# Attention on one core: sums of two units ago spread between the scores, own scores in four-row pieces, buffers in halves

## What is computed

```
q, k, v = 1x1 convolutions (256 x 256) of layernorm(x), as (n, 16 heads, 16 channels, row i, column w)
own      = sum_c q[c,i,j] * k[c,i,w]                     # per row i: 128 x 128
relative = Gq * sum_c q[c,i,j] * rq[c,j,w] + Gk * sum_c k[c,i,j] * rk[c,j,w]
weight   = softmax over w of (own + relative) / 16       # per head, image and row i: 128 x 128
out      = sum_w weight[i,j,w] * (Gv1 * v[c,i,w]) + sum_w weight[i,j,w] * (Gv2 * rv[c,j,w])
x = x + 1x1 convolution of out; then a mixture of 64 experts, each on its 8 best tokens
```

## Time and profile before

| | us |
|---|---|
| median of 3 runs | 8304.97 (8296.95 to 8308.47) |
| the profiled execution's own time | 8291.75 |
| its span | 8290.0 |
| TensorE busy in the span | 7187.2 (87%) |
| VectorE busy | 5176.6 (62%) |
| ScalarE busy | 4856.3 (59%) |
| GpSimd busy | 2457.0 (30%) |
| mean granted clock of TensorE | 0.749 of 2.4 GHz |

### The profile page before, as it was taken

One profiled execution on the slowest core, in us unless ns is written; L12 is line 12 of the kernel. 1 busy time (PEld: TensorE's weight loads), 2 busy tenths in 40 slices (PEclk: granted clock), 3 DMA queues, 4 the chain that ended last, 5 costly groups with the idle time before them and its releaser, 6 DMA issues. The chain is left out here.

```text
span 8290.0 us, 275612 instructions
## 1 busy us (share of the span) xinstructions
PE 7187.2 (87%) x106442; PEld 6044.4 (73%) x106442; DVE 5176.6 (62%) x20646; ACT 4856.3 (59%) x11427; POOL 2457.0 (30%) x1235
## 2 busy tenths in 40 slices
PE   4999999799999999999999899999999966766738
PEld 3555555689988888898899898898888932332338
DVE  5444444366666666666666666666666768988830
ACT  1444444577777777777777777777777733333410
POOL 0000000243443443444434444434434432322210
PEclk7999999666666666666666666666667688988855
DMA  7555555565655665655556656656656576766522
GB/s 217 203 203 204 204 204 197 113 112 100 112 103 98 113 107 101 107 99 107 101 106 112 102 100 109 109 99 110 105 100 109 92 232 203 265 201 202 208 74 99
DMA packets 1721071, 1148.11 MB, mean 138 GB/s; under 512 B 1143009, under 2 KB 1506145, under 8 KB 1703329
## 3 DMA queue, kind: packets, MB, share of 16 engines
q1 hardware_dynamic: 1530336, 842.56, 48.1%
q10 hardware_dynamic: 188352, 285.27, 9.3%
q0 software_dynamic: 1024, 2.09, 0.1%
HBM read 708.04 MB, written 421.56 MB: 136 GB/s over the span
## 5 line engine op out<-in xcount | busy, mean ns | idle before, releaser
L787 POOL TENSOR_TENSOR att_scores<-att_scores,att_inverse 128x1024 f32<-128x1024 f32 x1024 | 1966.8, 1934 | 2951.7 <-DVE att_inverse L722 2951.7
L660 ACT ACTIVATE att_scores<-att_scores,att_negmax 128x128 f32<-128x128 f32 x8192 | 2509.2, 399 | 67.6 <-issue 67.6
L737 DVE CUSTOM_DVE_ANT_0 att_scores<-att_ps,att_scores 128x128 f32<-128x128 f32 x8192 | 1780.8, 286 | 1066.7 <-PE att_ps L573 957.5
L560 PE MATMUL att_ps<-att_qk,att_rs 32*128 32x64 f32 x32768 | 1793.2, 380 | 155.6 <-ACT att_scores L652 114.2
L560 PEld LDWEIGHTS att_ps<-att_qk,att_rs 32*128 32x128 f32 x32768 | 1698.6, 299 | 196.2 <-ACT att_scores L652 142.5
L573 PE MATMUL att_ps<-att_own 16*128 16x128 f32 x16384 | 1541.6, 405 | 231.3 <-issue 224.1
L573 PEld LDWEIGHTS att_ps<-att_own 16*128 16x128 f32 x16384 | 1416.2, 300 | 268.9 <-issue 264.4
L652 ACT ACTIVATE att_scores<-att_ps 128x1024 f32<-128x1024 f32 x1024 | 992.4, 1021 | 1044.3 <-PE att_ps L560 1044.3
L720 DVE TENSOR_REDUCE att_total<-att_scores 128x8 f32<-128x1024 f32 x1024 | 1233.7, 1205 | 70.7 <-issue 70.7
L594 PE MATMUL att_ps<-att_scores,att_rv 128*16 128x64 f32 x32768 | 1249.6, 334 | 11.0 <-issue 10.8
L594 PEld LDWEIGHTS att_ps<-att_scores,att_rv 128*16 128x16 f32 x32768 | 1193.6, 127 | 24.5 <-issue 13.1
(11 more groups left out here) (146 smaller groups left out, 5276.0 us busy)
## 6 DMA issues: line engine op xcount, KB each, us to landing
qk<-proj_qk_out ACTq DMA_DIRECT2D x64, 2048.0 KB, 8.5
att_qk<-qk SPq DMA_DIRECT2D x512, 256.0 KB, 6.7
att_own<-qk SPq DMA_DIRECT2D x2048, 64.0 KB, 2.5
proj_x<-in_x_dram SPq DMA_DIRECT2D x128, 512.0 KB, 4.3
v_t<-proj_v_out ACTq DMA_DIRECT2D x64, 1024.0 KB, 11.3
att_vt<-v_t SPq DMA_DIRECT2D x128, 512.0 KB, 5.5
att_v<-att_att_v SPq DMA_DIRECT2D x512, 128.0 KB, 4.2
att_r<-att_att_r SPq DMA_DIRECT2D x512, 128.0 KB, 3.5
```

The costliest lines, as they stand in the source:

```text
L560: last = pe.matmul(ps[:, 4 + g, jj * IU:(jj + 1) * IU], rs[32 * g:32 * g + 32, t * JB + jj, :], qk[b][32 * g:32 * g + 32, :, t * JB + jj], ...
L660: last = act.activation(scores[v][:, i, :], scores[v][:, i, :], ACT.Exp, bias=negmax[v][:, i:i + 1], scale=-1.0)
L737: last = dve.tensor_tensor_reduce(out=scores[v][:, i, :], in0=ps[:, 2 * (p % 2) + r // 4, (r % 4) * W:(r % 4 + 1) * W], in1=scores[v][:, i ...
L787: pool.tensor_tensor(scores[v][:, rows, :], scores[v][:, rows, :], inverse[v][:, rows].unsqueeze(2).broadcast_to([P, PR, W]), ALU.mult).th ...
```

## The change

Every unit now has the same order of work on TensorE, and the sums in it are those of the unit two before. For each quarter t of a unit:

own piece 4t; relative round t, first half; v fill t, first half; own 4t+1; relative, third quarter; r fill t, first quarter; v fill t, second half; own 4t+2; relative, last quarter; r fill t, second and third quarter; own 4t+3; r fill t, last quarter.

An own piece now has 4 rows, all in the row group p % 4, and uses bank p % 2. Relative scores move to banks 2 to 5; all v sums go through bank 6 (read by VectorE alone) and all r sums through bank 7 (read by ScalarE). Both banks are cleared once at the start. `vt`, `att_v` and `att_r` are split in two halves with semaphores of their own, `rv` loads and their semaphores in four. Exponentials run two pieces behind the own scores, sums of exponentials two groups of eight rows behind. The scaling of the tables by GpSimd moves to later places, and `att_r` is stored as 8 runs of 16 columns in place of 4 of 32 (JT).

The core of the diff (left out: declarations, the load helpers and the unit's calls in SyncE's code at the start and the end):

```diff
-PR = 8
+PR = 4
 PIECES = IU // PR
+SR = 8
+SPIECES = IU // SR
-JT = JG
+JT = JG // 2
+STORES_G = JG // JT
...
# SyncE
             def unit(h, k, u, started, left):
                 if started >= 1:
                     sp.wait_ge(own_done, PIECES * u)
                     load_own(h, k, 1)
-                if started >= 2:
-                    store(*before(h, k, 2), u - 2)
-                if started >= 1:
-                    ph, pk = before(h, k, 1)
-                    later(sp, v_done, FILLS * (u - 1))
-                    load_v(ph, pk)
...
                 if left >= 2:
                     sp.wait_ge(rel_done, ROUNDS * u + ROUNDS)
                     load_qk(*after(h, k, 2))
+                if started >= 3:
+                    store(*before(h, k, 3), u - 3, 1)
+                if started >= 2:
+                    later(sp, v_done, FILLS * (u - 2))
+                    ph, pk = before(h, k, 2)
+                    load_v(ph, pk, 1)
+                    if pk == 0:
+                        later(sp, r_done, FILLS * (u - 2))
+                        load_rv(ph, 2)
+                        load_rv(ph, 3)
+                if k == UPH - 1 and left >= 1:
+                    load_relative(h + 1, 1)
...
                 if left >= 1:
                     sp.wait_ge(own_done, PIECES * u + PIECES // 2)
                     load_own(*after(h, k, 1), 0)
+                if started >= 2:
+                    store(*before(h, k, 2), u - 2, 0)
+                if started >= 1:
+                    ph, pk = before(h, k, 1)
+                    later(sp, v_done, FILLS * (u - 2) + FILLS // 2)
+                    load_v(ph, pk, 0)
...
# TensorE
             def own_scores(u, p):
+                half, g = p // (PIECES // 2), p % G
...
                 later(pe, added, PIECES * u + p - 1)
-                for r in range(4):
-                    for gg in range(2):
-                        g = 2 * (p % 2) + gg
-                        at = block16 * 4 + r
-                        last = pe.matmul(ps[:, g, r * W:(r + 1) * W], ...
+                for r in range(PR):
+                    at = (p // G) % (HROWS // 16) * PR + r
+                    last = pe.matmul(ps[:, p % 2, r * W:(r + 1) * W], ...
...
+            def unit(u, v, now, ahead, late, sums):
+                b, o = (v - 2) % BUFS, (v + 1) % 2
+                for t in range(FILLS):
+                    if now:
+                        own_scores(u, 4 * t)
+                    if ahead:
+                        relative(u + 1, o, t, (0, 1))
+                    if sums:
+                        sums_with_v(u - 2, b, t, (0, 1))
+                    if now:
+                        own_scores(u, 4 * t + 1)
+                    if ahead:
+                        relative(u + 1, o, t, (2,))
+                    if sums:
+                        sums_with_r(u - 2, b, t, (0,))
+                        sums_with_v(u - 2, b, t, (2, 3))
+                    if now:
+                        own_scores(u, 4 * t + 2)
+                    if ahead:
+                        relative(u + 1, o, t, (3,))
+                    if sums:
+                        sums_with_r(u - 2, b, t, (1, 2))
+                    if now:
+                        own_scores(u, 4 * t + 3)
+                    if sums:
+                        sums_with_r(u - 2, b, t, (3,))
...
# ScalarE
+            BEHIND = 2
+            def unit(u, v, now, ahead, late, sums):
+                for p in range(PIECES):
+                    if p < BEHIND:
+                        if late:
+                            exp_piece(u - 1, (v - 1) % BUFS, PIECES - BEHIND + p)
+                    elif now:
+                        exp_piece(u, v, p - BEHIND)
+                    if p % 4 == 3:
+                        if ahead:
+                            read_relative(u + 1, (v + 1) % BUFS, p // 4)
+                        if sums:
+                            read_r(u - 2, p // 4)
...
# VectorE
+                for p in range(PIECES):
+                    if now:
+                        add_and_largest(u, v, p)
+                    if sums and p % 4 == 2:
+                        read_v(u - 2, p // 4)
+                    if p % 2 == 1:
+                        k = p // 2 - BEHIND
+                        if k >= 0 and now:
+                            sums_of(u, v, k)
+                        elif k < 0 and late:
+                            sums_of(u - 1, (v - 1) % BUFS, SPIECES + k)
...
# GpSimd
-                        if k == UPH - 2 and not last and p in (2, 4):
-                            scale_relative(h + 1, p // 2 - 1)
+                        if k == UPH - 2 and not last and p == 6:
+                            scale_relative(h + 1, 0)
+                        if k == UPH - 1 and not last and p == 2:
+                            scale_relative(h + 1, 1)
```

More of the change, by code:

```diff
@@ L512, in unit @@
                     load_qk(*after(h, k, 2))
[L513 to L514 removed]
+                if started >= 3:
[10 more added lines that the diff above has]
+                    load_relative(h + 1, 1)
+                if k == UPH - 2 and left >= 2:
                     load_gain(h + 1)
@@ L577, in sums_with_v @@
[L577 to L581, removed]
+                for r in range(PR):
+                    at = (p // G) % (HROWS // 16) * PR + r
+                    last = pe.matmul(ps[:, p % 2, r * W:(r + 1) * W], own[half][32 * g:32 * g + HD, 1, at, :], own[half][32 * g:32 * g + HD, 0, at, :],
+                                     start=True, stop=True, tile_position=(32 * g, 0))
@@ L585, in sums_with_v @@
                                          start=True, stop=True, tile_position=(0, 32 * g))
[L586 to L593, removed]
-                        last = pe.matmul(ps[32 * g:32 * g + HD, bank, jj * IU:(jj + 1) * IU], rv[:, g * JG + b * JB + jj, :], scores[v][:, :, g * JG + b * JB + jj],
-                                         start=True, stop=True, tile_position=(0, 32 * g))
-                last.then_inc(r_done, 1)
@@ new lines, in sums_with_v, with sums_with_r @@
+                if 3 in quarters:
+                    last.then_inc(v_done, 1)
+            def sums_with_r(u, v, b, quarters):
+                if 0 in quarters:
+                    pe.wait_ge(rv_loaded[b], (u // UPH) * 16 + 16)
+                    if b == 0:
+                        pe.wait_ge(normed, SPIECES * u + SPIECES)
+                    later(pe, r_read, FILLS * u + b)
+                for x in quarters:
+                    for jj in range(x * JB // 4, (x + 1) * JB // 4):
+                        for g in range(G):
+                            j = g * JG + b * JB + jj
+                            last = pe.matmul(ps[32 * g:32 * g + HD, 7, jj * IU:(jj + 1) * IU], rv[:, j, :], scores[v][:, :, j],
+                                             start=True, stop=True, tile_position=(0, 32 * g))
+                if 3 in quarters:
+                    last.then_inc(r_done, 1)
@@ L640, in _ @@
+            pe.wait_ge(cleared, 1)
             for t in range(ROUNDS):
-                relative(0, 0, t)
+                relative(0, 0, t, (0, 1, 2, 3))
             units(pe, unit)
```

275 lines of the change are left out of this document (92 added, 183 removed).

## The result

The changed kernel took 9953.34 us (median of 4 runs, 9938.02 to 9991.55) beside 8300.96 us for the kernel before (4 runs, 8291.03 to 8308.47): 1.1998 times as long, 95% interval 1.1961 to 1.2035. That is 1652 us more, where 3060 were forecast. The direction and the range were right; the likeliest case, a low clock throughout, did not come. What came is the second rival, the swinging clock, priced at 10,020 and given a chance of 0.14.

The account below looks back on a forecast made before the run. TensorE was taken to bound the attention stage. At the low clock 128 units of 63.1 us plus 120 us of table waits make 8197 against 5137, +3060 us, so 11,365 us; range 8500 to 12,000.

Parts of the forecast that it names:

- the second rival: Attention clock swings, high half the time: 52.6 us a unit, +1716 us, 10,020 us; chance 0.14.
- Step 3: Attention clock: without long unbroken runs of sums it stays low (0.50); called the large term.
- Step 1: Own scores, each piece in one row group: records wait in turn, 25.2 us a unit low, 14.7 high.
- Step 2: Sums in sixteenths: 32 tiling changes a unit at 0.20 us low, 0.15 high, so 6.4 or 4.8 us.
- Step 4: TensorE's whole attention unit: 60.3 us low, 39.4 high with tiling changes; 63.1 and 42.2 with start-up and stalls.
- Step 5: ScalarE and VectorE swap v-sum reads in attention; both stay covered by TensorE: no added time.
- step 6: Relative scores' wait for ScalarE's read (100.6 us) goes: at most 0.8 us a unit, left out.
- step 8: SyncE's transfers, 38 DMAs a unit for 29: 7 to 8 us more, covered by a 63 us unit.
- step 9: Combine stage reads relative sums in 512-byte runs instead of 1024: taken as 0, at worst 60 us.
- Step 7: GpSimd's relative-table scaling at head's end stalls TensorE: two waits of about 4 us, 15 times, 120 us.
- The first rival: High clock holds through attention: 42.2 us a unit, +385 us, 8690 us; chance 0.12 (high and slower).
- The faster rival: High clock holds and loads run ahead hide tiling changes: 38.0 us a unit, -273 us, 8030; faster chance 0.14.

Follow-up runs that it names:

- e5: Changed kernel with sums dealt evenly, a quarter of v and of r sums behind each own piece; 11427.02 us, 1.3777 times the kernel before.
- e1: Changed kernel with each four-row own piece spread over two row groups, one bank each; 8773.01 us, 1.0578 times the kernel before.
- e3: Kernel before with each own piece issuing four matmuls of one row group, then four of the other, not alternating; 9031.67 us, ratio 1.0898.
- e7: Changed kernel with eight-row own pieces over two row groups and sums in eighths, 16 tiling changes a unit; 7900.54 us, 0.9529 times the kernel before.
- e6: Changed kernel with GpSimd's table scaling before pieces 4 and 1 instead of 6 and 2; 9805.48 us, 1.1815 times the kernel before.
- e8: e7 with the second half of values loaded first on SyncE and tables scaled earlier; 7759.19 us, 0.9356 times the kernel before.

## Why the prediction was right and where it failed

- **Step 3, the clock, failed.** It said that in the spread order the clock stays low for good. It was high 38% of the attention's time, about as much as before (36%). The stated range held the result because it reached over both clocks, not because the clock was understood. Taking 62.3 and 39.0 us a unit and the 370 us of stalls over 1 us (92, counted in the trace), (6783 - 370) = 62.3 n + 39.0 (128 - n) gives n = 61 low ones: half the units' work at either level, which is the rival priced at 10,020. The reasoning went wrong in making a long unbroken run of sums the condition: the changed order still has 48 records of r sums around one own piece at the end of each quarter, and with them the clock does rise (e5 takes them away and the forecast time comes, 11,427 beside 11,365). Half the units at the high level instead of none is 67 x 23.3 = 1560 us; the miss in time was 1412. Two smaller errors make about the difference: a low unit 2.0 us dearer, 256 us over 128, and stalls of 370 us for the 358 and 120 taken.
- **Step 1, one row group, was right.** 210 to 214 ns between records low and 107 to 112 high stand beside 197 and 115. e1 and e3 show that it costs time, 1180 and 746 us with what the clock did beside it. Its reason was only partly right. "Nothing runs beside it, since matmuls start in order" is refuted by the rows at 3003.04 and 3003.32: relative scores, which the program has behind the piece, start before its last own records do. Five slip in there; over the trace it is mostly three to seven where relative scores follow a piece and none where sums do, 3.6 in the mean. The trace of the kernel before had it too, which the prediction overlooked: two relative records start at 3138.18 and the last own record of the piece before them at 3138.39.
- **Step 2, changes of tiling, was right in kind and a little low:** 0.26 and 0.18 us measured, 0.20 and 0.15 taken, inside its bounds, 31.5 a unit. The Trainium skill's drain (TensorEngine Tiling (Array Packing), section Key Properties) was no overstatement.
- **Step 4, the sum, was right** (62.3 and 39.0 for 60.3 and 39.4), in part by luck, since errors cancel: own records and changes were dearer, v sums took 42 ns and r sums 31 ns at the low clock where 48 and 36 were taken, and relative scores slipped in beside own ones.
- **Step 5, step 6, step 8 and step 9 were right:** TensorE waits 0.7 us in all for `v_t` and for no store, 9.2 us for ScalarE's reads, and what stands behind the attention is as long as before (1625.5 us). Step 8 holds at 53 us a unit only: at e7's 37 the same queue costs 223.8 us.
- **Step 7, the tables, was mis-sized:** 182.3 us in 30 waits of 6.1, where 30 waits of 4 were taken. The scaling's 3.60 us was counted, and not what GpSimd still has to normalise ahead of it; e6, with less ahead of it, has 76.9 us.
- **The first rival (high clock holds, 8690)** did not come, with the high level in only half of the units. The faster rival (8030) needed changes under 0.11 us: refuted by 0.18. The gain of e7 and e8 comes with half as many changes.

## What to carry to other kernels

Price TensorE's work at both granted levels and then ask separately what share of the time each will have; the two lie far apart, here 23 us of 62 a unit, and a forecast that puts every unit on one level misses by that for each unit on the other. In the versions run here, spreading sums between score pieces paid only with pieces in two row groups, few changes of tiling and no waits for VectorE: with 16 changes a unit 5 to 6% faster than the kernel before, with 32 in two groups 4 to 6% slower, with 32 in one group 20% slower. After each gain read the waits again, since loads that 53 us a unit hid are late at 37.

## What the runs showed of the hardware that was not expected

- TensorE busy 7961.37 of 8268 us, with float32 own scores in one row group at a time and short runs of sums, is granted 0.50 in the mean of the stage (e5).
- A matmul of a free row group starts ahead of an earlier one that waits for its own: the relative record at 3003.04 before the own record at 3003.25. The Trainium skill (TensorE: Matmul & The Clock Gate, section The mechanism) has matmuls start strictly in the program's order; these rows disagree.
- Sums with relative v (128x64 moving) cost 30 to 36 ns a record at either clock, while own, relative and v records take little more than half the time at the high one (213 and 112, 52 and 28, 42 and 24 ns).
